# The order of work in a fused decoder's attention part: the context projection, the by-head products and two VectorE corrections moved

## The reference, cut to what matters

```
q = softmax(heads(x @ Wq.T + bq))        # 16 heads of 16 channels
k = softmax(heads(y @ Wk.T + bk))        # y: the context
v = heads(y @ Wv.T + bv)
D_inv = 1 / sum(q * sum(k over tokens))
kv = einsum('bhnd,bhne->bhde', k, v)
out = (q + (q @ kv) * D_inv) @ Wp.T + bp
x2 = layernorm(x1 + out)
```

## Time and profile before

| | us |
|---|---|
| median of 3 runs | 1837.73 (1837.53 to 1839.55) |
| the profiled execution's own time | 1839.56 |
| its span | 1837.8 |
| TensorE matmul, busy | 1733.5 (94%) |
| VectorE, busy | 1242.9 (68%) |
| ScalarE, busy | 972.6 (53%) |
| mean granted TensorE clock | 0.983 |
| attention part | about 701 to 897 of the span |

### The profile page before, as it was taken

How to read it: one execution, slowest core, us unless ns; L and a number is a source line. 1 busy time by engine, 2 the same in 40 slices (tenths; PEclk the granted TensorE clock), 3 DMA queues, 4 the chain that set the end, 5 groups by cost and what they waited for, 6 DMA issues and landing times.

```text
span 1837.8 us, 27207 instructions
## 1 busy us (share of the span) xinstructions
PE 1733.5 (94%) x10508; PEld 1519.3 (83%) x10508; DVE 1242.9 (68%) x1910; ACT 972.6 (53%) x1499; POOL 3.6 (0%) x26
## 2 busy tenths in 40 slices
PE   3599999999999998998999999999999999999997
PEld 1378888877888787888899889998999989999896
DVE  7999999999999865888554445454454544445446
ACT  4688898888889773444533333333333332333323
POOL 0000000000000000000000000000000000000000
PEclk9799999999999998999999999999999999999999
DMA  4000010001000002111111011100101001020001
GB/s 143 1 26 16 12 47 18 7 7 63 1 12 29 1 30 89 44 55 45 55 35 35 1 35 35 34 32 3 34 34 34 11 23 34 34 74 0 1 1 41
DMA packets 34702, 56.59 MB, mean 31 GB/s; under 512 B 3030, under 2 KB 20412, under 8 KB 33596
## 3 DMA queue, kind: packets, MB, share of 16 engines
q1 hardware_dynamic: 34620, 55.47, 9.3%
HBM read 51.79 MB, written 3.67 MB: 30 GB/s over the span
## 4 chain that ended last, share of the span: by engine, by line
PE 80%; DVE 15%; ACT 2%; issue 2%; DMA 0%; SPq 0%; ACTq 0%; DVEq 0%
PE fbank L1900 33%; PE fbank L1922 17%; PE pair L804 7%; PE pair L792 6%; PE pair L769 6%; PE pair L779 4%; PE proj L1394 2%; DVE st L263 1%; PE pair L759 1%; DVE kfl L416 1%; PE qbanks L1430 1%; PE abanks L1430 1%; DVE aa L365 1%; DVE bb L361 1%; DVE pp L347 1%
## 5 line engine op out<-in xcount | busy, mean ns | idle before, releaser
L1722 DVE TENSOR_TENSOR hf<-sil,fbank 128x512 f32<-128x512 f32 (+1 forms) x256 | 158.9, 621 | 479.4 <-PE fbank L1900 407.8
L1827 ACT ACTIVATE sil<-fbank 128x512 f32<-128x512 f32 (+1 forms) x256 | 139.3, 544 | 615.0 <-PE fbank L1900 614.9
L1900 PE MATMUL fbank<-xh,wh 128*128 128x512 f32 (+1 forms) x1024 | 289.9, 364 | 1.2 <-ACT sil L1827 1.2
L1900 PE MATMUL fbank<-xh,wl 128*128 128x512 f32 (+1 forms) x1024 | 288.9, 363 | 0.0
L1900 PE MATMUL fbank<-xl,wh 128*128 128x512 f32 (+1 forms) x1024 | 288.7, 363 | 0.0
L1922 PE MATMUL fbank<-wl,hh 128*128 128x256 f32 x896 | 250.3, 279 | 0.0
L1922 PE MATMUL fbank<-wh,hh 128*128 128x256 f32 x896 | 250.2, 279 | 0.0
L1922 PE MATMUL fbank<-wh,hl 128*128 128x256 f32 x896 | 250.1, 279 | 0.0
L1900 PEld LDWEIGHTS fbank<-xl,wh 128*128 128x128 f32 x1024 | 184.4, 189 | 30.8
L1900 PEld LDWEIGHTS fbank<-xh,wl 128*128 128x128 f32 x1024 | 184.4, 189 | 30.3
L1900 PEld LDWEIGHTS fbank<-xh,wh 128*128 128x128 f32 x1024 | 180.7, 189 | 27.8 <-ACT sil L1827 1.6
(11 more groups left out here) (227 smaller groups left out, 3048.5 us busy)
## 6 DMA issues: line engine op xcount, KB each, us to landing
raw<-in_w_gate SPq DMA_DIRECT2D x16, 512.0 KB, 3.8
raw<-in_w_up SPq DMA_DIRECT2D x16, 512.0 KB, 4.7
raw<-in_w_down SPq DMA_DIRECT2D x16, 512.0 KB, 5.8
raw<-in_w_ck SPq DMA_DIRECT2D x4, 1024.0 KB, 4.8
raw<-in_w_cv SPq DMA_DIRECT2D x4, 1024.0 KB, 4.8
raw<-in_ctx_t SPq DMA_DIRECT2D x4, 750.0 KB, 6.1
ct<-in_ctx_t SPq DMA_DIRECT2D x4, 750.0 KB, 4.9
x<-in_x SPq DMA_DIRECT2D x4, 448.0 KB, 7.0
```

The lines of the kernel that those rows point to most:

```text
L1722: dve.tensor_tensor(hf[i][:, 0:w], sil[i][:, 0:w], banks(e, t, f)[1][:, 0:w], ALU.mult).then_inc(hf_ready, 1)
L1827: act.activation(sil[f % 2][:, 0:w], banks(e, t, f)[0][:, 0:w], ACT.Silu).then_inc(sil_ready, 1)
L1900: ins = pe.matmul(banks(e, t, f)[k][:, 0:w], m[h][:, o:o + P], a[:, b, columns(c)], start=i == 0, stop=i == 3 * CB - 1)
```

## The change

On TensorE project is split into project_values (the first two value tiles) and project_rest. Both now stand at the head of the slot, ahead of the q products, the output products, the turn of x2 and the turn of q; with i = 0 the by-head products come between the two halves. On VectorE, in slots with i = 0, denominators(c2) and rsqrt(1, c1) go from behind low_context to ahead of k_normalise, in exchanged order; in slot 0 it is rsqrt(1, 0) alone. ScalarE's order is the same.

```diff
--- before.py
+++ after.py
@@ -1195,6 +1195,10 @@
                         block_diagonals(n - 1)
                     if i == 0 and c1 is not None:
                         add_input(c1)
+                    if i == 0 and c2 is not None:
+                        denominators(c2)
+                    if i == 0 and c1 is not None:
+                        rsqrt(1, c1)
                     if i == 2 and c1 is not None:
                         q_normalise(c1)
                     if i == 3 and c2 is not None:
@@ -1202,10 +1206,6 @@
                     k_normalise(n)
                     if n + 2 < B:
                         low_context(n + 2)
-                    if i == 0 and c1 is not None:
-                        rsqrt(1, c1)
-                    if i == 0 and c2 is not None:
-                        denominators(c2)
                     if i == 1 and c2 is not None:
                         attend(c2)
                     if i == 1 and c1 is not None:
@@ -1386,16 +1386,16 @@
             def add_bias(out, j, tokens):
                 return pe.matmul(out, onesr[:, 0:tokens], bias[:, j, :], start=False, stop=True)
 
-            def project(s):
-                def tile(out, t, cols):
-                    n = 0
-                    for a, w in ((cth, wkvh), (cth, wkvl), (ctl, wkvh)):
-                        for b in range(CB):
-                            ins = pe.matmul(proj[0:ST, out, :], a[s % 2][:, b, t * ST:(t + 1) * ST], w[:, b, cols],
-                                            start=n == 0, stop=n == 3 * CB - 1 and cols.start > 0)
-                            n += 1
-                    return ins if cols.start else add_bias(proj[0:ST, out, :], 0, ST)
-
+            def context_tile(s, out, t, cols):
+                n = 0
+                for a, w in ((cth, wkvh), (cth, wkvl), (ctl, wkvh)):
+                    for b in range(CB):
+                        ins = pe.matmul(proj[0:ST, out, :], a[s % 2][:, b, t * ST:(t + 1) * ST], w[:, b, cols],
+                                        start=n == 0, stop=n == 3 * CB - 1 and cols.start > 0)
+                        n += 1
+                return ins if cols.start else add_bias(proj[0:ST, out, :], 0, ST)
+
+            def project_values(s):
                 pe.wait_ge(ctl_ready, s + 1)
                 if s:
 
@@ -1403,18 +1403,20 @@
                 else:
                     pe.wait_ge(wkvl_ready, 1)
                 for t in range(2):
-                    ins = tile(STILES + 1 + t, t, slice(C, 2 * C))
+                    ins = context_tile(s, STILES + 1 + t, t, slice(C, 2 * C))
                 ins.then_inc(v01_done, 1)
+
+            def project_rest(s):
                 if s:
 
                     pe.wait_ge(v2_ready, s)
                     pe.wait_ge(arg_ready, s)
-                tile(STILES, 2, slice(C, 2 * C))
+                context_tile(s, STILES, 2, slice(C, 2 * C))
                 if s == 0:
                     pe.wait_ge(bias_ready, 1)
-                tile(2, 2, slice(0, C)).then_inc(v2_done, 1)
+                context_tile(s, 2, 2, slice(0, C)).then_inc(v2_done, 1)
                 for t in range(2):
-                    ins = tile(t, t, slice(0, C))
+                    ins = context_tile(s, t, t, slice(0, C))
                 ins.then_inc(proj_done, 1)
 
             def turn(banks, src, done):
@@ -1486,7 +1488,8 @@
             gate_up, experts = g["expert"]["tensor"](pe)
             last = GROUPS - 1
             pe.wait_ge(const_set, 4)
-            project(0)
+            project_values(0)
+            project_rest(0)
             pe.wait_ge(w_in, 32)
             pe.wait_ge(bv_in, 16)
             for b in range(CB):
@@ -1494,6 +1497,12 @@
             ins.then_inc(pbias_done, 1)
             for n in range(B):
                 i, c1, c2 = stage(n)
+                if n + 1 < B:
+                    project_values(n + 1)
+                if i == 0 and c2 is not None:
+                    attend(c2)
+                if n + 1 < B:
+                    project_rest(n + 1)
                 if i == 1 and c1 is not None:
                     pe.wait_ge(xt_ready, c1 + 1)
                     tokens_out(qbanks, xt, wq, 1, q_done)
@@ -1506,10 +1515,6 @@
                         pe.wait_ge(g["x2t_ready"], TURNS.index(n - 1) + 1)
                     pe.wait_ge(q_ready, c1 + 1)
                     turn(qbanks, q[c1 % 2], q_turned)
-                if n + 1 < B:
-                    project(n + 1)
-                if i == 0 and c2 is not None:
-                    attend(c2)
                 if n == B - 1:
                     gate_up(0, 0, 0)
                     gate_up(0, 0, 1)
```

## The result

The changed kernel takes 1847.8 us (1846.92 to 1848.75, 5 runs) against 1838.6 us (1837.53 to 1841.05, 5 runs) for the kernel before: ratio 1.0046, 95% interval 1.0035 to 1.0056. The medians differ by 9.2 us; by the ratio it is 8.5 us. 6.5 were forecast. The profiled execution has a span of 1845.2 us (before 1837.8), +7.4; it took 1846.92 us and is the fastest of its five.

A forecast was written before the change was run, and what follows sets the result against it. TensorE is busiest, but VectorE ends last around i = 3 and i = 0. The slots' +5.5 us plus 1.0 for the clock make +6.5, taking 1837.73 to 1844.2 us; range 1836.7 to 1850.0.

The forecast's parts named there:

- The walk: Slots (one context each) replayed in the new queue order with old durations; stretches between keys_values starts K(n) sum to +5.5 us.
- slot 4: K(3) to K(4): q's copy on ScalarE goes ahead of the v copies that k_arguments and project_values wait for; +1.5 us.
- slot 5: K(4) to K(5), i = 1: the q products' 1.01 us copy wait and 0.3 of slower restart go; -1.2 us.
- slots 6, 10 and 14: Slots with i = 2: the other copy wait goes, but project_rest waits 1.1 us for later arguments; 0.
- slot 11: The later turn of x2 in slot 10 holds up ScalarE, k_arguments(11) and the projection; K(11) 13.1 behind K(10), +4.6 us.
- slot 15: The later turn of x2 in slot 14 delays v_out(15), k_arguments(15) and the silu chain to K(15); +2.9 us.
- The signs to look for: In the changed profile: no copy waits, K(0) about 716.9, 1 us kcm waits, K(11) some 13 us behind K(10).
- The clock: TensorE's granted clock falling to half after waits in slots 2, 10, 11 and 15: 1.0 us, bounds 0 and 5.1.
- rival C: TensorE's clock falls to half three times on the path: +10.6 us, 1848.3; chance 0.20.
- The start: First slots: K(0) +1.5 us, K(1) -2.5 with the clock back at full, K(2) unmoved behind a 10.2 us chain; zero.
- A: A wash: slots 10 and 14 cost half of the 7.5 us, slot 4 nothing; +0.3 us, 1838; chance 0.22.
- B: TensorE is the bound throughout, so its copy waits and reciprocal waits come back; -7.5 us, 1830.2; chance 0.13.

The follow-up runs named there:

- experiments 1 and 2: The changed kernel with the turn of x2 at the head of slots 10 and 14 (1836.79 us), slot 10 alone (1840.67) or slot 14 alone (1842.84).
- experiment 6: The kernel before with only project_values moved ahead of the q and output products: 1830.33 us; with the turn of x2 also at the slot head: 1829.44 us.
- fill_slot11: The changed kernel with two times 18 added products keeping TensorE busy through its two waits in slot 11: 1845.59 us, ratio 1.0037 to the kernel before.
- experiment 5: The run of fill_slot11: added products in slot 11 of the changed kernel, 1845.59 us.
- turn10_first: The changed kernel with the turn of x2 at the head of slot 10 only: 1840.67 us, ratio 0.9997 to the kernel before.
- turn14_first: The changed kernel with the turn of x2 at the head of slot 14 only: 1842.84 us, ratio 1.0018 to the kernel before.
- turns_first: The changed kernel with the turn of x2 at the head of slots 10 and 14: 1836.79 us, ratio 0.9982 to the kernel before.

## Why the prediction was right

**The direction and the mechanism.** Slower was forecast at 0.65, with the turn of x2 as what decides. The two slots with that turn lose 5.0 and 4.1 us, all the rest together -1.3; and with the turn alone moved to the head the kernel is faster than the one before. This is shown by experiments 1 and 2, and with the late turn's size by experiment 6: what the prediction had, 6.6 us from the turn's start to k_arguments(11), measured 6.61.

**The walk, term by term.** Forecast and measured: slots 0 to 3 together 0 and -0.1; slot 4 +1.5 and +1.7; slot 5 -1.2 and -1.3; slot 7 +0.15 and +0.1; slot 8 +0.2 and +0.3; slot 9 -1.35 and -1.2; slots 6, 10 and 14 0 and 0; slot 11 +4.6 and +5.0; slot 12 +0.25 and +0.7; slot 13 -1.55 and -1.6; slot 15 +2.9 and +4.1. The sum is +5.5 and +7.8. Where the clock stays at full the walk is nearer still: fill_slot11 has +4.6, +0.3 and +2.9 in slots 11, 12 and 15, and +6.0 at K(15). The signs to look for came as written: K(0) at 716.7 (716.9), the 1 us wait for kcm in three slots, 2.33 us ahead of project_values(12) (2.5), K(11) 13.5 behind K(10) (13.1), K(8) to K(9) 11.1 (11).

**The clock, the term that was mis-sized.** I took 1.0 us, between 0 and 5.1, "as VectorE ends last behind most of them". The clock fell in all three places, which is rival C's case. In slot 15 no VectorE work covers it: silu's release to K(15) took 2.72 us (883.80 to 886.52), and 1.51 before, so 1.2 us lie on the path. TensorE of the kernel before:

```profile
...
877.17 0.74 PE L1900 MATMUL fbank<-xh,wh 128*128 128x512 f32 x2 [1.22 <-ACT sil L1827]
...
878.68 1.50 PE L1482 MATMUL kvp<-v,k 125*128 125x129 f32 x12
...
```

In fill_slot11, at full clock, it was 1.50 again (883.18 to 884.68). In slot 11 it was 0.4, by experiment 5. In slot 12, behind a slower projection with its v copies, it was another 0.4, by the same. Together 2.0, not 1.0, of the 2.3 us by which the marks exceed the walk. The fall in slot 3 cost another 1.5 and is hidden in the start's zero, below. Rival C's 10.6 charged all three in full, and is closer to the median's 9.2 than the 6.5; the measured time lies between them. The profiled pair differs by 7.4; the rest of the 9.2 is in which executions were profiled, the slower side of the runs before and the fastest after.

**The start** came out at zero for a reason other than mine. K(1) was 4.0 us earlier, not 2.5, as the clock was back at 719.9, ahead of the projection and not in it. K(2) was 1.6 earlier, where the walk had it unmoved. Then, behind the wait of 2.21 us ahead of K(2), the clock fell once more, K(2) to K(3) took 8.4 us instead of 6.85, and the gain was gone at K(3):

```profile
...
716.67 2.95 PE L1484 MATMUL kvp<-v,k 125*128 125x129 f32 x12 [4.59 <-DVE k L1103]
...
739.30 1.98 PE L1484 MATMUL kvp<-v,k 125*128 125x129 f32 x12 [2.21 <-DVE k L1103]
...
```

The wait ahead of K(0) grew from 3.02 to 4.59 us, 1.57 for the 1.5 walked. That the start adds up to zero is partly luck. Three more profiles with the same order up to K(3) (turn10_first, turn14_first, turns_first) have K(3) at -0.1, +1.3 and +1.6 against the kernel before, and fill_slot11 at 0.0. In the two with zero the second fall came at 735.8 us, ahead of K(2), where it only shortened TensorE's wait for VectorE from 2.21 to 0.7 us, and K(2) to K(3) took 6.85; in the two others it came behind K(2), as in the changed kernel.

**The rivals.** A asked that slot 10 and 14 cost half: they cost more than walked. B, TensorE as the bound everywhere, failed at the place where I had put its test: the q products' wait went, and VectorE had no slack in slots 0 and 3 of a group. TensorE did have 10 us to give (experiment 6), by an edit that leaves VectorE's inputs nearly where they were. The Trainium skill, Perfetto Trace Analysis (Identifying the Most-Contended Engine), says to optimise the engine with the highest occupancy first. This case agrees that TensorE was worth the work: two edits aimed at the same waits of it gave -10 and +9 us. Which of them it would be was read from the chain between the engines.

## What to carry to other kernels

Before a block is moved ahead of a product that waits, list what the delayed instructions release, and what stands in program order behind their consumers on the other engines: here a 0.8 us turn (the transpose of finished x2 rows) moved by 4 us held up ScalarE, then VectorE, then TensorE, and cost more than the seven waits that the move took away. Move only as much as covers the wait (1.4 us of products for 1.01 us), and leave what feeds the second-busiest engine where it was. A walk through the slots with the durations of the old trace found each slot from 4 on to within 0.5 us, except slot 15, where the clock fell on the path.

## What the runs showed that I had not expected

The clock's falls are not fixed to a wait. The 2.37 us wait ahead of silu in slot 15 took the clock to half in the changed kernel, and a wait of 2.36 us in the same place did not in fill_slot11 (884 to 886 at 1.00 there). In the profiled turns_first the clock was at half for 6.8 us in slot 4, after waits of 0.23 and 1.01 us:

```profile
...
756.00:762.00 6.00, 6.00 (x31) 0.50 0.00 0
...
```

K(3) to K(4) is 14.2 us there, 2.4 more than in the changed kernel. The runs of turns_first spread from 1833.94 to 1838.53 us, those of turn10_first from 1836.57 to 1841.31, 11 runs each. What a fall costs depends on where it lies: nothing in slot 2 (turn10_first), 1.2 us in slot 15, 1.5 in slot 3, 2.4 for the long one in slot 4. So a single profile of such a kernel carries one or two falls more or less, worth 0 to 2.4 us, and a difference of that size between two profiles isn't the edit's until the marks around it say so.
